# Attention weights times v as 64x64 blocks on separate rows and columns of the array, and one chunk's transposes moved ahead of it

## The reference, cut to what matters

```python
h = layernorm(x) * (1 + ca) + sa
q, k, v = split(h @ w_qkv + b_qkv)                  # 8 heads of 64
scores = einsum('bhld,bhle->bhde', q, k) / 8        # 64 x 64 for each head, summed over the 2048 tokens
attn = softmax(scores, -1)
out = einsum('bhld,bhde->bhle', v, attn)            # heads joined again: 2048 x 512
out = out @ w_fc + b_fc + h
x = x + ga * (norm(out) * gamma + beta)
h = layernorm(x) * (1 + cb) + sb
x = x + gb * (sigmoid(xr @ W_r.T) * (square(relu(xk @ W_k.T)) @ W_v.T))   # xr, xk: h mixed with its token before
```

## Time and profile before

| what | value |
|---|---|
| median of 3 runs | 682.86 us (682.77 to 684.41) |
| time of the profiled execution | 681.41 us |
| its span, first to last instruction | 679.5 us |
| mean granted TensorE clock | 0.994 of full speed |
| TensorE busy | 653.2 us (96%) |
| VectorE, ScalarE, GpSimd busy | 567.5, 457.0, 288.0 us |

### The profile page before, as it was taken

The page is one execution under the profiler, slowest core; times in us unless marked ns, Lnnn a source line. Parts: engine busy times, 40 slices in busy tenths (PEclk is TensorE's granted clock), DMA queues, the critical chain, the costliest instruction groups (busy, mean ns, idle before and its releaser), DMA issues. The chain is left out here.

```text
span 679.5 us, 12488 instructions
## 1 busy us (share of the span) xinstructions
PE 653.2 (96%) x3968; PEld 535.5 (79%) x3968; DVE 567.5 (84%) x1328; ACT 457.0 (67%) x983; POOL 288.0 (42%) x499
## 2 busy tenths in 40 slices
PE   8987899999999999999999999999999999999896
PEld 6776777888869887889868888788878898697665
DVE  5994988889788988899798897889888997858973
ACT  1423686776957688666967779567876769667662
POOL 5272632753228242662318532382327543214320
PEclk9979999999999999999999999999999999999999
DMA  8749336584945867294855759268663727538225
GB/s 317 240 151 207 125 101 124 93 181 110 202 100 91 223 121 183 42 186 135 191 95 101 188 116 205 70 127 205 138 147 66 135 72 171 102 74 186 31 33 92
DMA packets 90985, 93.04 MB, mean 137 GB/s; under 512 B 4224, under 2 KB 89000, under 8 KB 90960
## 3 DMA queue, kind: packets, MB, share of 16 engines
q0 software_dynamic: 33264, 33.03, 33.0%
q1 hardware_dynamic: 55344, 55.97, 25.8%
q10 hardware_dynamic: 2352, 3.73, 1.5%
HBM read 42.84 MB, written 33.10 MB: 112 GB/s over the span
## 5 line engine op out<-in xcount | busy, mean ns | idle before, releaser
L478 POOL TENSOR_TENSOR rs<-ve,neg_half 128x4 f32<-128x4 f32 x32 | 38.9, 1215 | 183.5 <-DVE ve L944 183.5
L1424 PE MATMUL work<-mx,w_k_t 128*128 128x512 f32 x244 | 109.9, 592 | 0.0
L1407 PE MATMUL work<-w_r_t,mx 128*128 128x256 f32 x464 | 105.9, 381 | 0.0
L717 ACT ACTIVATE z<-x,nm,rs 128x256 f32<-128x256 f32 x128 | 66.3, 593 | 48.6 <-POOL nm L480 48.6
L1407 PEld LDWEIGHTS work<-w_r_t,mx 128*128 128x128 f32 x464 | 85.8, 190 | 11.2 <-DVE y L1008 0.3
L1354 PE MATMUL gram<-z 128*128 128x256 f32 (+1 forms) x512 | 89.1, 327 | 0.0
L1354 PEld LDWEIGHTS gram<-z 128*128 128x128 f32 x512 | 79.8, 191 | 6.6
L1424 PEld LDWEIGHTS work<-mx,w_k_t 128*128 128x128 f32 x244 | 46.3, 190 | 46.0 <-issue 42.0
L1238 PE MATMUL att<-m_lo,z_hi 128*128 128x256 f32 x248 | 74.2, 299 | 4.2 <-DVE t_buf L923 2.2
L1238 PE MATMUL work<-wvf_lo,k_hi 128*128 128x256 f32 x248 | 72.3, 291 | 5.9 <-DVE k_lo L999 3.1
L1239 PE MATMUL att<-m_hi,z_hi 128*128 128x256 f32 x248 | 70.0, 282 | 0.0
(11 more groups left out here) (186 smaller groups left out, 1595.4 us busy)
## 6 DMA issues: line engine op xcount, KB each, us to landing
x_in<-in_L_attn_x_dram SPq DMA_DIRECT2D x32, 512.0 KB, 5.0
x<-rows SPq DMA_DIRECT2D x32, 512.0 KB, 3.5
x<-in_L_attn_x_dram POOLq DMA_DIRECT2D x32, 512.0 KB, 8.8
out_dram<-x SPq DMA_DIRECT2D x31, 512.0 KB, 5.1
out_dram<-y POOLq DMA_DIRECT2D x29, 512.0 KB, 5.9
rows<-row_scratch SPq DMA_DIRECT2D x16, 128.0 KB, 5.2
rows<-row_scratch SPq DMA_DIRECT2D x8, 256.0 KB, 4.0
wqkv_sb<-in_L_attn_w_qkv_dram ACTq DMA_DIRECT2D x1, 1536.0 KB, 9.7
```

Of the source, the lines that this page charges most:

```text
L717: ins = nc.scalar.activation(z2[:, t], x2[:, j, t], ACT.Identity, bias=nm_2[:, s, t:t + 1], scale=rs_2[:, s, t:t + 1])
L1407: ins = mm(r_banks(alone)[q][:, (t % 2) * D:(t % 2 + 1) * D], mixed(j)[0][:, ch, tile], w_r_t[:, ch], start=(ch == 0), stop=(ch == KD - 1))
L1424: ins = mm(k_banks(alone)[dh][:], w_k_t[:, ch, rows_dh], mixed(j)[1][:, ch], start=(ch == 0), stop=(ch == KD - 1))
```

## The change

`wv_attn` issues two matmuls of 64 rows by 64 columns for each pair of heads, one for each diagonal block, in place of one of 128 x 128. Block g takes rows 64g to 64g + 63 of the array and columns 64g to 64g + 63. The two write different banks: block 0 of pair p goes to bank p // 2, block 1 to the other one. So the lower halves of the two banks are swapped against before, and the output weights are loaded with their lower 64 partitions swapped in the same way, by three DMAs in place of one. `pv_done` is raised by 2 at the last of the eight matmuls. The waits of `wv_attn` are now a function of their own, `wait_attn`, and in `row_steps` `turn_z2(b, 3)` stands between it and the matmuls.

```diff
-                act.dma_start(wfc_c[:], w_fc.rearrange("(n p) d -> p n d", p=P)).then_inc(wfc_loaded, 16)
+                fc_v = w_fc.rearrange("(n g p) d -> g p n d", g=2, p=DX)
+                act.dma_start(wfc_c[0:DX], fc_v[0]).then_inc(wfc_loaded, 16)
+                for q in range(2):
+                    act.dma_start(wfc_c[DX:P, 2 * q:2 * q + 2], fc_v[1, :, 2 - 2 * q:4 - 2 * q]).then_inc(wfc_loaded, 16)
...
-                dve.wait_ge(wfc_loaded, 16)
+                dve.wait_ge(wfc_loaded, 48)
...
-            def wv_attn(b):
-
+            def wait_attn(b):
                 pe.wait_ge(attn_ready, b + 1)
                 pe.wait_ge(wv_ready, b + 1)
+
+            def wv_attn(b):
                 for p in range(NP):
-                    ins = mm(att[p // 2][:, (p % 2) * D:(p % 2 + 1) * D], attn[:, p], wv_aug[:, p], start=True, stop=True)
-                    if p % 2:
-                        ins.then_inc(pv_done, 1)
+                    for g in range(2):
+                        rows_g = slice(g * DX, (g + 1) * DX)
+                        ins = mm(att[p // 2 ^ g][rows_g, (p % 2) * D:(p % 2 + 1) * D], attn[rows_g, p, rows_g], wv_aug[rows_g, p],
+                                 start=True, stop=True)
+                ins.then_inc(pv_done, 2)
...
                 scores(n)
                 ffn_r(b, 2)
                 ffn_k(b, 2)
+                wait_attn(n)
+                turn_z2(b, 3)
                 wv_attn(n)
-                turn_z2(b, 3)
                 make_m(n)
                 ffn_out(b, 2)
...
             turn_ffn()
+            wait_attn(0)
             wv_attn(0)
             pe.wait_ge(fc_ready, 1)
             make_m(0)
```

## The result

| kernel | runs | median us | lowest to highest | profiled execution, its span |
|---|---|---|---|---|
| before | 5 | 682.86 | 681.5 to 684.41 | 681.41, 679.5 |
| changed | 5 | 694.43 | 693.38 to 695.18 | 694.3, 692.5 |

The ratio is 1.0168 (95% interval 1.0153 to 1.0184): the change costs 11.6 us by the medians, where 13.5 were forecast. 696.4 us was the forecast, 690 to 702 its range.

The account below looks back on a forecast made before the run. TensorE's stream of matmuls was taken to bound the kernel. 7 x 1.81 + 0.8 = 13.5 us on the profiled 681.41 gave 694.9; with the median 1.45 us above that execution, the forecast was 696.4 us, range 690 to 702.

Parts of the forecast that it names:

- Transposes first and into the form, 0.97: After `ffn_k`, transposes take 0.88 us and the change to 64x64 form 0.09, so the first products start at 0.97.
- The products' last start 1.72 after the first: Blocks side by side, 16 product records fill 8 + 1 slots of 0.215 us; last starts 1.72 us after the first.
- First copy 0.41 after the last start, both copies 1.10: ScalarE's first copy starts 0.41 us after the last product's start; two copies back to back take 0.50 and 0.60.
- TensorE behind a real wait 0.14, refill 0.07: `make_m` starts 0.14 us after the copies; its first record after idling adds 0.07 us.
- 1.81 us for each row: Delay at `make_m`: 1.74 us later start plus 0.07, in each of seven rows.
- All of it moves with TensorE: Behind `make_m`, VectorE has no backlog to swallow the delay; nothing given back for the 0.5 us k_lo wait.
- Prologue 0.8, the loads nothing: Before the first `attention`: 0.8 us for slot, form and copies; two further DMA issues count nothing, bound 0.8.
- blocks in series: Rival at the products: blocks don't run side by side, last record 1.51 us later in 8 places, 708.5 us; chance 0.11.
- not slower: Rival: products so cheap that the k_lo wait takes in `make_m`'s 0.37 us delay, 683 us; chance 0.04.
- The clock's fall: Rival: the clock falls through `make_m`, 3.4 us more a row, 720 us; chance 0.03.

Follow-up runs that it names:

- number 4: The changed kernel with its products sorted, block 0 of all four pairs and then block 1 of all four: 704.83 us, ratio 1.0318.
- number 1: The kernel before with only the eight transposes moved ahead of its 128x128 products, loads and counts as before: 689.96 us, ratio 1.0116.
- number 9: The changed kernel with the second bank's copy on VectorE, placed ahead of the next row's last statistics: 691.18 us, ratio 1.0122.
- number 8: The kernel before with the output weights loaded by three DMAs in natural order: 684.25 us over 12 runs, ratio 1.0020.
- number 6: The changed kernel with the second bank's copy on VectorE, ahead of its k_lo of chunk 2 but behind next-row statistics: 704.52 us, ratio 1.0326.
- 10: The kernel before with 64x64 products, one bank per pair, one count per bank, one load, seven transposes behind the products: 685.42 us, ratio 1.0041.
- number 2: The changed kernel with one of the eight transposes ahead of the 64x64 products and seven behind them: 689.14 us, ratio 1.0089.
- 3: The changed kernel with the output weights loaded by one DMA as before, their lower 64 partitions not swapped: 693.13 us, ratio 1.0157.
- 5: The changed kernel with both blocks of a pair in one bank and one load in natural order: 693.63 us, ratio 1.0164.

## Why the prediction was right, point by point

The mechanism, the place and the order of size were right. Its steps, in its own count from the end of `ffn_k`:

- *Transposes first and into the form, 0.97.* Measured 0.96. The 0.09 us that the scores showed carried over to the new form.
- *The products' last start 1.72 after the first.* This term was too large by 0.16: measured 1.56. I let instructions start in the order of the list, which gave a slot in which only one block works. There is none, the 16 records start in eight pairs. The idea that the list's order holds between the blocks was wrong as such, by number 4. Number 4 shows that TensorE pairs records that are further apart than neighbours. That blocks on separate rows run side by side at all, for which no row of before spoke, held in all eight places.
- *First copy 0.41 after the last start, both copies 1.10.* Measured 0.43 and 1.09. Number 1 confirms the part of one copy, number 9 the gain of one copy less.
- *TensorE behind a real wait 0.14, refill 0.07.* Both too large: 0.05, and 0.02 (`make_m` lasts 3.72, before 3.70). I had taken them from a prologue row, where the changed kernel again shows 0.15, and from a row with another wait.
- *1.81 us for each row.* 1.49 measured. The three terms above make up the 0.32.
- *All of it moves with TensorE.* A row's period is 1.55 us longer, no less than at the place (only row 0, with 1.16, gives some back at another wait), and the wait for k_lo is 3.2 us where it was 3.1. VectorE's wait for `make_m` is 1.4 us in six rows (it was 1.0), so it had no backlog to swallow the delay.
- *Prologue 0.8, the loads nothing.* The weak step. From the first product to `make_m(0)` it takes 4.02 us (50.92 to 54.94) where it was 2.90, 1.1 in place of 0.8. In the rows, at full clock, the same stretch takes 3.13 us, and 2.58 with 128x128 products (number 1), so the change itself is worth 0.55; the other 0.57 are the lower clock, under which more of the products ran (0.50 from 50 to 52 us, before 1.00). And the loads are not free: about 1.4 us by number 8, where I kept 0.8 as a bound and counted none. I priced an issue by the old one's 0.40 us; those of 64 partitions took 0.63 to 0.70. And I thought that VectorE's 1.1 us of slack would take it in, while TensorE's z_lo chain had less.

Too much in the rows (2.2 us) and too little in the prologue (about 1.8) cancel in the profiled execution: 694.9 forecast, 694.3 measured. That it comes so close is luck. The median lies 2.0 us below its forecast, since the five runs of the changed kernel lie around its profiled execution, and I had added 1.45 us for the three of before.

Of the rivals, blocks in series didn't come, and "not slower" neither. The clock's fall didn't come in this kernel, with the 1.2 us of idle time, but number 6 shows that it stood near: with 2.0 us behind the same transposes and products it came at three of five `make_m` of an execution, for 1.7 us each. It was cheaper than the 3.4 us a row that I had given it. My argument against it, the 2.0 us of idle time at 56 to 58 us that left the clock at 1.00, was one execution's luck: the same pause of 2.02 us in front of the first `attention` stands in all twelve profiled executions, and in three of them (numbers 4, 8 and 10) the clock fell behind it.

The parts add up over the experiments: 0.85 us a row for the lost cover with one late copy (number 1), 0.29 for the form (number 10), together 1.14, and 0.35 remain for the first bank's count being raised only at the end. That last term is a difference and was not run alone; number 2 against number 10 (3.33 and 2.89) shows it as 0.44 where one copy is partly covered.

## What to carry to other kernels

Before moving a small block of work on the engine that bounds the kernel, ask what runs under it elsewhere: here eight transposes of 0.88 us hid the second copy almost to the hundredth (the first lay under the products). Without them it cost 0.69 us of idle time a row, and 1.19 once the first copy had to wait for the last product too. Two half-size products in place of one with zeros beside its blocks win nothing here, as the pairs follow each other at 0.21 us like the single records before, and a count raised only at the last of them delays every copy behind it. The gain lay in the one wait that the profile did show: turning two steps round in front of it won 0.64%.

## What the runs showed of the hardware

- Two 64x64 blocks on the array's diagonal run side by side, their starts 6 ns apart, into two banks or into one (1.94 and 1.95 us for 16 records). Sorted by block, 4 of 8 records still overlapped, and the second block's first product started ahead of the first block's last (number 4).
- The change from 128x128 transposes to 64x64 products costs 0.09 us (0.96 from the first transpose to the first product, 0.87 in number 1).
- A DMA issue on ScalarE took 0.63 to 0.70 us for 64 partitions, where one for 128 of the same load took 0.40.
- The granted clock fell from 1.00 to the lower level, 0.50, behind some pauses of TensorE of about 2 us and not behind others of the same length and place: at three of five `make_m` with 2.02 to 2.03 us in number 6, and in front of the first `attention` (2.02 us) in three of twelve profiled executions, two of them (numbers 4 and 10) with 64x64 products and one (number 8) with full ones before `make_m(0)`. Behind the 28 pauses of 1.17 to 1.19 us at `make_m` in the changed kernel and in numbers 3, 4 and 5 it never fell. In the prologue, behind matmuls of 8 columns, it fell at about 14 us in seven of the twelve, with pauses from 0.85 to 1.68 us. What tells the cases apart the runs don't show; one execution without a fall does not show a pause to be harmless.
